# A cross-attention kernel on one core: GpSimd adds beta in two parts, and VectorE takes a residual ahead of a centring

## The chip, the cores and the metric

The kernel runs on 1 core of one Trainium2 chip. The metric is device time in microseconds (us). All times of the trace are counted from the start of the span of one profiled execution.

## The reference

```python
def _L0_xattn_ref(emb, latent, Wq, bq, Wk, bk, Wv, bv, gamma, beta):
    EPS = 1e-06
    q = jnp.einsum('bte,ef->btf', emb, Wq) + bq
    k = jnp.einsum('bml,le->bme', latent, Wk) + bk
    v = jnp.einsum('bml,le->bme', latent, Wv) + bv
    scale = 1.0 / jnp.sqrt(jnp.asarray(E, dtype=q.dtype))
    w = jnp.einsum('bte,bme->btm', q, k) * scale
    w = jax.nn.softmax(w, axis=1)
    pred = jnp.einsum('btm,bme->bte', w, v)
    x = pred + emb
    mu = jnp.mean(x, axis=-1, keepdims=True)
    var = jnp.var(x, axis=-1, keepdims=True)
    return (x - mu) * jax.lax.rsqrt(var + EPS) * gamma + beta
```

`emb` is x, 16 batches of 512 x 512 float32; `latent` is the context, 16 batches of 120 x 256. The softmax runs over the 512 tokens of a batch. The last three lines are a layer norm over the 512 features of a token.

## The kernel before

A batch's 512 tokens lie on 128 partitions as four units of 128 tokens x 512 features. Each engine has its own program, written out by hand; semaphores are all that ties them together, and an engine that waits holds up everything behind it in its program.

The loop has one step for each batch. In step s TensorE works on three batches at once:

- it turns x of batch s (L371; x must have landed), which ScalarE copies to `xT` (L501);
- it multiplies the probabilities of batch s-2 by its v, four products of 128 tokens each (L390), into the banks a, b, a, b. Products 1 and 2 stand between the two halves of the turning, 3 and 4 behind it. Product 4 writes the bank that VectorE's second residual reads, and waits for it;
- it multiplies contexts with the combined query and key matrix into `cg_ps` (L352, from which ScalarE makes `gT`, L496), computes v of batch s-1 (L363, which waits for the third residual, since it writes bank a), in steps 3, 5, 7, 9 and 11 turns a pair of contexts (L336, which waits for `gT`), and computes the scores of batch s (L400).

In the same step VectorE makes the softmax of batch s-1 ready (L680 to L689), takes the four residuals of batch s-2 (L721: product + x, with a sum), scales the softmax (L694, L696), makes the low half of the probabilities (L700, `prob_low`, which waits for ScalarE's high half, L513, `prob_high`), copies v (L706) and takes the statistics of unit 4 (L727, L729). Unit 4 of batch s-3 it normalises by itself: `center` (L746) subtracts the mean and multiplies by gamma, `rescale` (L754) multiplies by the inverse deviation and adds beta. In the first steps it also computes key products, `key_dot` (L675) and `key_sum` (L670).

Units 1 to 3 take another way. ScalarE squares them (L528) and GpSimd turns the sums into an inverse deviation and a `shift` (L940 to L958, `finish_statistics`). A step later ScalarE's `normalise` (L534) applies both: the first unit between the exponential (L506) and `prob_high`, the second and third behind the copies of `xT`. GpSimd multiplies each by gamma (L925, `times_gamma`) and adds beta to all three in one instruction (L931, `plus_beta`). Then its statistics of the next batch follow. So GpSimd's program for one batch is gamma, gamma, gamma, beta, statistics.

All DMAs are issued by SP, in one queue. In its loop a store of a batch (L295) waits for GpSimd (`pool_out`) and VectorE (`dve_out`), and the next load of x (L262), into a ring of four buffers, stands behind that store in SP's program. In step s that load is x of batch s+1. Stores leave from a ring of three buffers.

The last two batches divide the units otherwise (`pool_units`: 1 and 2 on GpSimd, the rest on VectorE) and are stored unit by unit.

Of the kernel before, what the change touches and what calls it, by code (L numbers as in the profile page):

```python
# [5 lines left out]
P = 128  # L6
# [3 lines left out]
ALU = mybir.AluOpType  # L10
# [5 lines left out]
ORING = 3  # L16
# [22 lines left out]
def cross_attention(nc, x, ctx_in, Wq, bq, Wk, bk, Wv, bv, gamma, beta, out):  # L39
    B, T, E = x.shape  # L40
# [11 lines left out]
    def pool_units(b):  # L52

        return {B - 2: 1, B - 1: 2}.get(b, 3)

    def units_before(b):
        return sum(pool_units(i) for i in range(b))
# [15 lines left out]
    def dve_units_before(b):  # L73
        return sum(dve_units(i) for i in range(b))
# [5 lines left out]
    with ExitStack() as stack:  # L80
        def sb(name, shape, dt=F32):
            return stack.enter_context(nc.sbuf_tensor(name, shape, dt))
# [4 lines left out]
        def sem(name):  # L87
            return stack.enter_context(nc.semaphore(name))
# [13 lines left out]
        beta_all = sb("beta_all", [P, E])  # L102
# [27 lines left out]
        obuf = sb("obuf", [P, ORING, RJ, E])  # L130
# [119 lines left out]
        pool_gamma = sem("pool_gamma")  # L250
        pool_out = sem("pool_out")
# [7 lines left out]
        @block.sync  # L259
        def _(sp):  # L260
            def load_x(b):
                sp.dma_start(xbuf[:, b % XRING], x[b].rearrange("(p j) e -> p j e", j=RJ)).then_inc(x_in[b % XRING], 16)  # L262

            def load_ctx(g):
                first = g * IN_GROUP
                sp.dma_start(ctx_nat[:, first:first + IN_GROUP, 0:L],
                             ctx_in[first:first + IN_GROUP].rearrange("b m l -> m b l")).then_inc(ctx_in_sem[g], 16)

            sp.dma_start(wk_nat[:], Wk.rearrange("(c p) f -> p c f", p=P)).then_inc(wk_in, 16)
            for h in range(2):  # L270
                sp.dma_start(wq_nat[:, 2 * h:2 * h + 2], Wq.rearrange("(c p) f -> p c f", p=P)[:, 2 * h:2 * h + 2])\
                    .then_inc(wq_in[h], 16)
            load_ctx(0)
            sp.dma_start(bk_all[:], bk.partition_broadcast(P)).then_inc(bk_in, 16)
            sp.dma_start(bq_all[:], bq.partition_broadcast(P)).then_inc(bq_in, 16)
            load_x(0)
            load_ctx(1)
            sp.dma_start(wv[:], Wv.rearrange("(c p) e -> p c e", p=P)).then_inc(wv_in, 16)
            load_ctx(2)
            load_ctx(3)  # L280
            sp.dma_start(bv_all[:], bv.partition_broadcast(P)).then_inc(bv_in, 16)
            load_x(1)
            load_x(2)
            sp.dma_start(gamma_all[:], gamma.partition_broadcast(P)).then_inc(gamma_in, 16)
            sp.dma_start(beta_all[:], beta.partition_broadcast(P)).then_inc(beta_in, 16)
            load_x(3)

            for s in range(4, B + 2):
                if s < B:
                    sp.wait_ge(y_done, RJ * (s - 4) + RJ)  # L290
                    load_x(s)
                b = s - 4
                sp.wait_ge(pool_out, b + 1)
                sp.wait_ge(dve_out, dve_units_before(b + 1))
                sp.dma_start(out[b].rearrange("(p j) e -> p j e", j=RJ), obuf[:, b % ORING])\  # L295
                    .then_inc(stored[b % ORING], 16)

            for b in range(B - 2, B):
                for j in (2, 0, 3, 1) if b == B - 1 else (1, 2, 3, 0):
                    sp.wait_ge(last_out[b - B + 2][j], 1)  # L300
                    sp.dma_start(out[b].rearrange("(p j) e -> p j e", j=RJ)[:, j], obuf[:, b % ORING, j])\
                        .then_inc(last_stored, 16)
            for k in range(ORING):
                sp.wait_ge(stored[k], 16 * len(range(k, B - 2, ORING)))
            sp.wait_ge(last_stored, 16 * 2 * RJ)
# [322 lines left out]
        def _(dve):  # L628
# [63 lines left out]
            def softmax_scale(b):  # L692
                dve.wait_ge(probs_done, b + 1)
                dve.reciprocal(s_rec[:], s_sum[:]).then_inc(rec_done, 1)  # L694
                dve.wait_ge(rec_done, b + 1)
                dve.tensor_scalar(s_by[:], s_rec[:], PROB_SCALE, None, ALU.mult).then_inc(by_done, 1)  # L696
# [17 lines left out]
            def residual(b, j):  # L714
                dve.wait_ge(pv_done, RJ * b + j + 1)
                if j == 0:
                    if b >= ORING:
                        dve.wait_ge(stored[b % ORING], 16 * (b // ORING))
                    if b >= 2:
                        dve.wait_ge(shift_done, b - 1)  # L720
                dve.scalar_tensor_tensor(obuf[:, b % ORING, j, :], y_bank(b, j), back_y[:], xbuf[:, b % XRING, j, :],  # L721
                                         ALU.mult, ALU.add, accum_out=y_sum[:, b % 2, j:j + 1]).then_inc(y_done, 1)
# [116 lines left out]
            for s in range(2, B):  # L839
                y, norm = s - 2, s - 3  # L840
                softmax_bias(s - 1)
                residual(y, 0)
                softmax_scale(s - 1)
                if norm >= 0:
                    center(norm, RJ - 1, norm + 1)
                residual(y, 1)
                probs_to_low(s - 1)
                residual(y, 2)
                residual(y, 3)
                if norm >= 0:  # L850
                    rescale(norm, RJ - 1)
                copy_v(s - 1)
                statistics(y)
                if s % 2 == 1 and (s + 3) // 2 < PAIRS:
                    ctx_to_low((s + 3) // 2)
                v_to_low(s - 1)
                if s == B - 1:
                    copy_v(s)
                    v_to_low(s)
                if s < IN_GROUP:  # L860
                    key_dot(s)
                if s - 1 in (1, 2, 3):
                    key_sum(s - 1)
# [24 lines left out]
        def _(pool):  # L888
# [36 lines left out]
                    pool.tensor_tensor(obuf[:, b % ORING, j, :], obuf[:, b % ORING, j, :], gamma_all[:], ALU.mult)\  # L925
                        .then_inc(pool_gamma, 1)

            def plus_beta(b):
                n = pool_units(b)
                pool.wait_ge(pool_gamma, units_before(b + 1))  # L930
                pool.tensor_tensor(obuf[:, b % ORING, 0:n, :], obuf[:, b % ORING, 0:n, :],  # L931
                                   beta_all[:].unsqueeze(1).broadcast_to([P, n, E]), ALU.add)\
                    .then_inc(pool_out if b < B - 2 else last_out[b - B + 2][0], 1)

            def finish_statistics(b):
# [25 lines left out]
            for s in range(2, B + 1):  # L961
                if s == 3:
                    key_multiply(s)
                if s >= 3:
                    times_gamma(s - 3)
                    plus_beta(s - 3)
                finish_statistics(s - 2)
            finish_statistics(B - 1)
            times_gamma(B - 2)
            plus_beta(B - 2)  # L970
            for j in range(pool_units(B - 1)):
                pool.wait_ge(norm_done, units_before(B - 1) + j + 1)
                pool.tensor_tensor(obuf[:, (B - 1) % ORING, j, :], obuf[:, (B - 1) % ORING, j, :], beta_all[:],
# [22 lines left out]
```

## Time and profile before

| | |
|---|---|
| median of 3 runs | 228.85 us (227.89 to 231.82) |
| profiled execution | 228.07 us |
| its span | 226.2 us |
| TensorE matmul busy | 190.5 us, 84% |
| VectorE busy | 169.3 us, 75% |
| ScalarE busy | 162.7 us, 72% |
| GpSimd busy | 142.0 us, 63% |
| TensorE's granted clock, mean | 0.957 of full speed |

The busy shares are means over an opening of some 40 us, the loop, and a tail from about 203 us on. In a timeline a row is one instruction, or several alike that follow one another: its start, its length, the engine, the line of the kernel, the operation, output <- inputs, sizes, and the count. In brackets stands how long the engine was idle before it, and what ended that. Matmuls are pipelined, so the row of one may reach into the next.

### The profile page before, as it was taken

Reading aid. Unit: us, or ns where it says so; the run is one execution under the profiler, and the core shown is the slowest. Engines: PE = TensorE matmul, PEld = TensorE weight load, DVE = VectorE, ACT = ScalarE, POOL = GpSimd, SP = SyncE. Lnnn points to the kernel's source line nnn. Section 1 sums busy time; section 2 is a strip of 40 time slices with the busy share of each in tenths; the row PEclk is TensorE's granted clock in tenths of the full one; section 3 lists DMA queues with packets and bytes.
Section 4 is the critical chain, followed back from the end, with each engine's and each line's share of the span. In section 5 each row is a group of like instructions: output and inputs, shape, how many; then the busy total and the mean of one; then the engine's idle time right before and its main releaser. Section 6 shows DMA issues by size and latency. Waiting matters only on the chain.

```text
span 226.2 us, 3278 instructions
## 1 busy us (share of the span) xinstructions
PE 190.5 (84%) x1003; PEld 117.6 (52%) x1003; DVE 169.3 (75%) x403; ACT 162.7 (72%) x336; POOL 142.0 (63%) x149
## 2 busy tenths in 40 slices
PE   6994998899996999999999999999999969696100
PEld 6993655465554565656565656555656535342000
DVE  0698138979899896959695969586958686879891
ACT  2745638378968797978797879787978876748730
POOL 1010005103994969696969696969696969698991
PEclk9999599999999999999999999999999999999855
DMA  5999940014018090909090909090909090404175
GB/s 220 315 313 250 398 198 1 3 14 172 0 81 293 0 346 28 352 22 351 23 355 17 352 19 351 23 336 36 348 26 352 19 351 25 185 0 187 67 294 197
DMA packets 9277, 39.14 MB, mean 173 GB/s; under 512 B 812, under 2 KB 2732, under 8 KB 5420
## 3 DMA queue, kind: packets, MB, share of 16 engines
q1 hardware_dynamic: 9260, 38.93, 49.0%
q8 instruction: 8, 0.13, 0.2%
q14 instruction: 9, 0.07, 0.1%
HBM read 22.15 MB, written 16.78 MB: 172 GB/s over the span
## 4 chain that ended last, share of the span: by engine, by line
PE 40%; POOL 16%; DVE 14%; ACT 9%; issue 8%; DMA 7%; SPq 2%; POOLq 1%; ACTq 0%; DVEq 0%
PE s_ps L400 16%; DMA ctx_nat<-in_ctx 7%; POOL obuf L925 7%; PE xT_ps L371 6%; POOL obuf L931 5%; PE a_ps L363 5%; PE a_ps L390 4%; PE b_ps L390 4%; DVE obuf L721 4%; PE cg_ps L352 4%; ACT xT L501 3%; ACT obuf L534 2%; POOL rstd L954 2%; ACT prob_part L513 2%; DVE obuf L746 2%
## 5 line engine op out<-in xcount | busy, mean ns | idle before, releaser
L925 POOL TENSOR_TENSOR obuf<-obuf,gamma_all 128x512 f32<-128x512 f32 x43 | 54.2, 1276 | 24.9 <-ACT obuf L534 24.9
L400 PE MATMUL s_ps<-xT,gT 128*120 128x512 f32 x128 | 58.9, 604 | 0.0
L931 POOL TENSOR_TENSOR obuf<-obuf,beta_all 128x1536 f32<-128x1536 f32 (+1 forms) x15 | 49.6, 3306 | 1.2
L501 ACT ACTIVATE xT<-xT_ps 128x512 f32<-128x512 f32 x64 | 34.6, 593 | 17.3 <-PE xT_ps L371 17.3
L534 ACT ACTIVATE obuf<-obuf,shift,rstd 128x512 f32<-128x512 f32 x43 | 33.4, 813 | 9.0 <-POOL shift L958 9.0
L371 PEld LDWEIGHTS xT_ps<-ident,xbuf 128*128 128x128 f32 x256 | 30.1, 142 | 15.1 <-issue 8.0
L371 PE MATMUL xT_ps<-ident,xbuf 128*128 128x128 f32 x256 | 34.0, 275 | 3.8 <-ACT xT L501 3.8
L400 PEld LDWEIGHTS s_ps<-xT,gT 128*120 128x120 f32 x128 | 23.5, 188 | 25.6 <-issue 23.7
L528 ACT ACTIVATE square_junk<-obuf,y_sum 128x512 f32<-128x512 f32 x46 | 32.8, 716 | 0.0
L390 PE MATMUL b_ps<-v_part,prob_part 120*128 120x512 f16 x90 | 24.5, 381 | 4.9 <-DVE obuf L721 4.9
L680 DVE TENSOR_REDUCE s_max<-s_ps 120x1 f32<-120x512 f32 x16 | 11.0, 689 | 20.3 <-PE s_ps L400 20.3
L390 PE MATMUL a_ps<-v_part,prob_part 120*128 120x512 f16 x90 | 24.4, 379 | 1.7 <-DVE v_part L711 0.9
L363 PE MATMUL a_ps<-wv_part,ctxT 128*120 128x512 f16 x90 | 22.0, 381 | 3.4 <-DVE obuf L721 3.1
L721 DVE SCALAR_TENSOR_TENSOR obuf<-a_ps,back_y,xbuf 128x512 f32<-128x512 f32 x30 | 22.4, 745 | 3.0 <-PE a_ps L390 3.0
L721 DVE SCALAR_TENSOR_TENSOR obuf<-b_ps,back_y,xbuf 128x512 f32<-128x512 f32 x30 | 22.3, 745 | 0.0
L352 PE MATMUL cg_ps<-ctxT,qk_part 128*128 128x240 f16 x156 | 18.1, 266 | 0.0
L390 PEld LDWEIGHTS b_ps<-v_part,prob_part 120*128 120x128 f16 x90 | 7.6, 97 | 19.1 <-DVE obuf L721 11.7
L706 DVE SCALAR_TENSOR_TENSOR a_ps<-a_ps,onto_v,bv_scaled 120x512 f32<-120x512 f32 x15 | 11.4, 758 | 8.2 <-PE a_ps L363 8.2
L954 POOL TENSOR_TENSOR rstd<-var_eps,minus_half 128x4 f32<-128x4 f32 x16 | 16.3, 1020 | 1.3 <-POOL var_eps L940 0.2
L352 PEld LDWEIGHTS cg_ps<-ctxT,qk_part 128*128 128x128 f16 x156 | 15.2, 98 | 3.5
L363 PEld LDWEIGHTS a_ps<-wv_part,ctxT 128*120 128x120 f16 x90 | 11.2, 133 | 10.1 <-issue 4.0
L700 DVE SCALAR_TENSOR_TENSOR prob_part<-s_ps,s_by,prob_part 120x512 f16<-120x512 f32 x16 | 12.0, 750 | 4.0 <-ACT prob_part L513 3.7
(142 smaller groups left out, 277.2 us busy)
## 6 DMA issues: line engine op xcount, KB each, us to landing
xbuf<-in_x SPq DMA_DIRECT2D x16, 1024.0 KB, 7.4
out<-obuf SPq DMA_DIRECT2D x14, 1024.0 KB, 4.8
out<-obuf SPq DMA_DIRECT2D x8, 256.0 KB, 2.8
ctx_nat<-in_ctx SPq DMA_DIRECT2D x4, 480.0 KB, 14.0
wq_nat<-in_L_xattn_Wq SPq DMA_DIRECT2D x2, 512.0 KB, 5.0
wk_nat<-in_L_xattn_Wk SPq DMA_DIRECT2D x1, 512.0 KB, 3.7
wv<-in_L_xattn_Wv SPq DMA_DIRECT2D x1, 512.0 KB, 14.3
bk_all<-in_L_xattn_bk SPq DMA_DIRECT2D x1, 256.0 KB, 7.6
```

What stands on the lines that cost most here:

```text
L352: mm = pe.matmul(ps[:, i * 2 * M:(i + 1) * 2 * M], qk_part[:, of_w, c, e * P:(e + 1) * P], ctxT[:, pair % 3, of_ctx, c, :], start=(n == 0) ...
L363: mm = pe.matmul(v_bank(b)[0:M, :], ctxT[:, b // 2 % 3, of_ctx, c, at:at + M], wv_part[:, of_w, c, :], start=(n == 0), stop=(n == len(step ...
L371: mm = pe.transpose(xT_ps[e % 2][:, j, :], xbuf[:, b % XRING, j, e * P:(e + 1) * P], ident[:])
L390: mm = pe.matmul(y_bank(b, j), prob_part[:, b % 2, of_p, j * P:(j + 1) * P], v_part[:, b % 2, of_v, :], start=(n == 0), stop=(n == len(PAS ...
L400: mm = pe.matmul(s_ps[0:M, :], gT[:, b // 2 % 2, e, b % 2 * M:(b % 2 + 1) * M], xT[:, e, :], start=(e == 0), stop=(e == EC - 1))
L501: act.activation(xT[:, e, :].rearrange("p (j q) -> p j q", q=P), xT_ps[e % 2][:], ACT.Copy)\
L528: act.activation(junk[:, j], obuf[:, b % ORING, j, :], ACT.Square, scale=-float(E), bias=y_sum[:, b % 2, j:j + 1], accum_out=square_sum[:, ...
L534: act.activation(obuf[:, b % ORING, j, :], obuf[:, b % ORING, j, :], ACT.Identity, bias=shift[:, b % 2, j:j + 1], scale=rstd[:, b % 2, j:j ...
L721: dve.scalar_tensor_tensor(obuf[:, b % ORING, j, :], y_bank(b, j), back_y[:], xbuf[:, b % XRING, j, :], ALU.mult, ALU.add, accum_out=y_sum ...
L925: pool.tensor_tensor(obuf[:, b % ORING, j, :], obuf[:, b % ORING, j, :], gamma_all[:], ALU.mult)\
L931: pool.tensor_tensor(obuf[:, b % ORING, 0:n, :], obuf[:, b % ORING, 0:n, :], beta_all[:].unsqueeze(1).broadcast_to([P, n, E]), ALU.add)\
L954: pool.tensor_tensor(rstd[:, k], var_eps[:], minus_half[:], ALU.pow).then_inc(rstd_done, 1)
```

## The change

GpSimd's addition of beta, which was one instruction for all three units of a batch, becomes two: units 1 and 2 at the old place, and unit 3 behind the next batch's statistics. `pool_out` counts both, so SP waits for twice the count. On VectorE the second residual and the centring change places.

```diff
@@ SP, the loop over stores and loads
                 b = s - 4
-                sp.wait_ge(pool_out, b + 1)
+                sp.wait_ge(pool_out, 2 * (b + 1))
                 sp.wait_ge(dve_out, dve_units_before(b + 1))
@@ VectorE, step s
                 softmax_scale(s - 1)
+                residual(y, 1)
                 if norm >= 0:
                     center(norm, RJ - 1, norm + 1)
-                residual(y, 1)
                 probs_to_low(s - 1)
@@ GpSimd
-            def plus_beta(b):
-                n = pool_units(b)
-                pool.wait_ge(pool_gamma, units_before(b + 1))
-                pool.tensor_tensor(obuf[:, b % ORING, 0:n, :], obuf[:, b % ORING, 0:n, :],
-                                   beta_all[:].unsqueeze(1).broadcast_to([P, n, E]), ALU.add)\
+            def plus_beta(b, first, end):
+                pool.wait_ge(pool_gamma, units_before(b) + end)
+                pool.tensor_tensor(obuf[:, b % ORING, first:end, :], obuf[:, b % ORING, first:end, :],
+                                   beta_all[:].unsqueeze(1).broadcast_to([P, end - first, E]), ALU.add)\
                     .then_inc(pool_out if b < B - 2 else last_out[b - B + 2][0], 1)
@@ GpSimd, its loop
                 if s >= 3:
                     times_gamma(s - 3)
-                    plus_beta(s - 3)
+                    plus_beta(s - 3, 0, 2)
                 finish_statistics(s - 2)
+                if s >= 3:
+                    plus_beta(s - 3, 2, 3)
             finish_statistics(B - 1)
             times_gamma(B - 2)
-            plus_beta(B - 2)
+            plus_beta(B - 2, 0, 1)
```

GpSimd's program in the middle of the loop, before: from one batch's gamma to the next batch's. The names in brackets are the semaphores that an instruction waits for.

```order
L925 TENSOR_TENSOR obuf<-obuf,gamma_all 128x512 [waits norm_done] x3
L931 TENSOR_TENSOR obuf<-obuf,beta_all 128x1536 [waits pool_gamma]
L940 TENSOR_SCALAR var_eps<-square_sum 128x3 [waits squares_done]
L947 TENSOR_SCALAR neg_mean<-y_sum 128x3 [waits dve_out,centered,norm_done]
L951 TENSOR_TENSOR var_eps<-mean_var,eps_all 128x1 [waits aggr_done]
L954 TENSOR_TENSOR rstd<-var_eps,minus_half 128x4 [waits var_ready]
L958 TENSOR_TENSOR shift<-neg_mean,rstd 128x3 [waits mean_negated,rstd_done]
L925 TENSOR_TENSOR obuf<-obuf,gamma_all 128x512 [waits norm_done] x3
```

The same place after the change (the file is one line shorter there):

```order
L925 TENSOR_TENSOR obuf<-obuf,gamma_all 128x512 [waits norm_done] x3
L930 TENSOR_TENSOR obuf<-obuf,beta_all 128x1024 [waits pool_gamma]
L939 TENSOR_SCALAR var_eps<-square_sum 128x3 [waits squares_done]
L946 TENSOR_SCALAR neg_mean<-y_sum 128x3 [waits dve_out,centered,norm_done]
L950 TENSOR_TENSOR var_eps<-mean_var,eps_all 128x1 [waits aggr_done]
L953 TENSOR_TENSOR rstd<-var_eps,minus_half 128x4 [waits var_ready]
L957 TENSOR_TENSOR shift<-neg_mean,rstd 128x3 [waits mean_negated,rstd_done]
L930 TENSOR_TENSOR obuf<-obuf,beta_all 128x512 [waits pool_gamma]
L925 TENSOR_TENSOR obuf<-obuf,gamma_all 128x512 [waits norm_done] x3
```

The statistics moved ahead of one third of beta, and that third moved between them and the next batch's gamma.

VectorE's program in a step of the loop, as a piece of the difference, from the scaling of the softmax to the third residual:

```order
 L696 TENSOR_SCALAR s_by<-s_rec 120x1
-L746 SCALAR_TENSOR_TENSOR obuf<-obuf,mean_var,gamma_ps 128x512
-L721 SCALAR_TENSOR_TENSOR obuf,y_sum<-b_ps,back_y,xbuf 128x512
+L721 SCALAR_TENSOR_TENSOR obuf,y_sum<-b_ps,back_y,xbuf 128x512
+L746 SCALAR_TENSOR_TENSOR obuf<-obuf,mean_var,gamma_ps 128x512
 L700 SCALAR_TENSOR_TENSOR prob_part<-s_ps,s_by,prob_part 120x512
 L721 SCALAR_TENSOR_TENSOR obuf,y_sum<-a_ps,back_y,xbuf 128x512
```

The residual from bank b (L721) and the centring (L746) changed places; both stand ahead of `prob_low` (L700) as before.

## Rows read from the trace of the kernel before

**Rows 1.** Timeline of GpSimd in step 8, and its second gamma seven steps later.

```profile
115.40 1.27 POOL L925 TENSOR_TENSOR obuf<-obuf,gamma_all 128x512 f32<-128x512 f32 x1 [0.93 <-ACT obuf L534]
117.65 2.51 POOL L925 TENSOR_TENSOR obuf<-obuf,gamma_all 128x512 f32<-128x512 f32 x2 [0.98 <-ACT obuf L534]
120.24 3.46 POOL L931 TENSOR_TENSOR obuf<-obuf,beta_all 128x1536 f32<-128x1536 f32 x1
123.78 0.20 POOL L940 TENSOR_SCALAR var_eps<-square_sum 128x3 f32<-128x3 f32 x1
...
125.59 0.20 POOL L958 TENSOR_TENSOR shift<-neg_mean,rstd 128x3 f32<-128x3 f32 x1
...
196.75 2.51 POOL L925 TENSOR_TENSOR obuf<-obuf,gamma_all 128x512 f32<-128x512 f32 x2 [0.98 <-ACT obuf L534]
```

**Rows 2.** Timeline of ScalarE in step 8: the first normalise, then the other two.

```profile
114.51 0.81 ACT L534 ACTIVATE obuf<-obuf,shift,rstd 128x512 f32<-128x512 f32 x1 [0.24 <-POOL shift L958]
...
116.75 1.52 ACT L534 ACTIVATE obuf<-obuf,shift,rstd 128x512 f32<-128x512 f32 x2
```

**Rows 3.** Timeline of TensorE: where steps 5, 8 and 15 begin, a wait, four products.

```profile
77.85 1.04 PE L371 MATMUL xT_ps<-ident,xbuf 128*128 128x128 f32 x8
...
108.00 0.60 PE L336 MATMUL cg_ps<-ident,ctx_nat 120*128 120x120 f32 x4 [0.33 <-ACT gT L496]
...
111.88 1.04 PE L371 MATMUL xT_ps<-ident,xbuf 128*128 128x128 f32 x8
...
113.40 0.81 PE L390 MATMUL b_ps<-v_part,prob_part 120*128 120x512 f16 x3
114.05 1.04 PE L371 MATMUL xT_ps<-ident,xbuf 128*128 128x128 f32 x8
114.92 0.81 PE L390 MATMUL a_ps<-v_part,prob_part 120*128 120x512 f16 x3
116.06 0.82 PE L390 MATMUL b_ps<-v_part,prob_part 120*128 120x512 f16 x3 [0.32 <-DVE obuf L721]
...
190.03 1.04 PE L371 MATMUL xT_ps<-ident,xbuf 128*128 128x128 f32 x8
```

**Rows 4.** Timeline of VectorE: centring and second residual in step 8, prob_low in step 15.

```profile
114.58 0.75 DVE L746 SCALAR_TENSOR_TENSOR obuf<-obuf,mean_var,gamma_ps 128x512 f32<-128x512 f32 x1
115.25 0.74 DVE L721 SCALAR_TENSOR_TENSOR obuf<-b_ps,back_y,xbuf 128x512 f32<-128x512 f32 x1
...
195.03 0.75 DVE L700 SCALAR_TENSOR_TENSOR prob_part<-s_ps,s_by,prob_part 120x512 f16<-120x512 f32 x1 [0.88 <-ACT prob_part L513]
```

**Rows 5.** SP's x(10) load; then x loads' us to landing: x(7,9,10,11,13,15).

```profile
124.11 0.43 SPq L262 DMA_DIRECT2D xbuf<-in_x  x1
...
xbuf<-in_x SPq DMA_DIRECT2D x1, 1024.0 KB, 7.7
...
xbuf<-in_x SPq DMA_DIRECT2D x1, 1024.0 KB, 7.5
...
xbuf<-in_x SPq DMA_DIRECT2D x1, 1024.0 KB, 6.9
...
xbuf<-in_x SPq DMA_DIRECT2D x1, 1024.0 KB, 8.4
...
xbuf<-in_x SPq DMA_DIRECT2D x1, 1024.0 KB, 8.6
...
xbuf<-in_x SPq DMA_DIRECT2D x1, 1024.0 KB, 7.3
```

**Rows 6.** Timeline of steps 3 and 4: a GpSimd, a VectorE and two TensorE rows.

```profile
62.58 3.45 POOL L931 TENSOR_TENSOR obuf<-obuf,beta_all 128x1536 f32<-128x1536 f32 x1
...
64.06 2.26 DVE L675 SCALAR_TENSOR_TENSOR key_junk<-ctx_nat,w_row 120x257 f32<-120x257 f32 x1
...
69.35 0.82 PE L390 MATMUL a_ps<-v_part,prob_part 120*128 120x512 f16 x3 [0.79 <-DVE obuf L721]
...
71.23 0.82 PE L390 MATMUL b_ps<-v_part,prob_part 120*128 120x512 f16 x3 [1.06 <-DVE obuf L721]
```

## The prediction

> **What bounds the kernel now.** I read the page first (engine shares and the chain that ended last), then the timelines of GpSimd, ScalarE, TensorE and VectorE over step 8 of the loop, and last the DMA queue. The page shows TensorE as the busiest engine, but the timelines show that it does not set the pace. Write T(s) for the moment at which TensorE starts to turn x of batch s; T(8) is 111.88 [rows 3]. In step 8 ScalarE's first normalise starts at 114.51, and its bracket says that it waited 0.24 us for GpSimd's `shift` [rows 2]. The second normalise starts 2.24 later, at 116.75. GpSimd's second and third gamma units start at 117.65, 0.90 behind that. Beta starts at 120.24, 2.59 later, and lasts 3.46; the statistics start at 123.78 and `shift` ends at 125.79, 2.01 later [rows 1]. Then the next step's normalise can go. That ring is 2.24 + 0.90 + 2.59 + 3.54 + 2.01 = 11.28 us, and 0.03 more to the next normalise make 11.31. From 117.65 to the same instruction seven steps later, at 196.75, are 79.10 us, so 11.30 each [rows 1]: the ring of GpSimd and ScalarE sets every step. TensorE runs into it: in every step its fourth product waits for VectorE's second residual. Products that wait for nothing follow one another at 0.65 us (113.40 to 114.05), the fourth started 1.14 behind the third (114.92 to 116.06), so it stood 0.49; in steps that turn a pair of contexts it stood another 0.33 for ScalarE's gT [rows 3]. So TensorE alone would need two steps in about 22.60 - 0.98 - 0.33 = 21.3 us.
>
> **Beta in two parts.** A unit of 128x512 costs 1.27, read from gamma, which is the same operation [rows 1], three together 3.46, so each unit beyond the first costs 1.09 and two units 2.36. The ring loses 1.10 us and becomes about 10.2 a step, shorter than TensorE's 10.6. The third unit costs 1.27, so GpSimd works 0.17 more per batch. It lies behind `shift`, where GpSimd stood idle 0.93 us for the first normalise [rows 1]; the rest, 0.3 us, only moves the first gamma unit, and between the first and second gamma there is another 0.98 us of idle time [rows 1]. It costs nothing while that idle time is there; without it, 1.27 a step, which would undo the saving.
>
> What is late next is the store, since `pool_out` now counts two per batch, and SP issues the next x load behind that store. Before, the load that follows was issued at 124.11, 0.41 behind the end of beta and T(8) + 12.23 [rows 5]. After, with `shift` no longer late, the first normalise starts at T + 2.63 - 0.24 = 2.39, the second at 4.63, the gamma pair at 5.53, beta at 8.12, its two units end at 10.48, the statistics start 0.08 later and end at 12.57, the third unit ends 1.27 + 0.08 later at 13.92, and the load is issued at T + 14.33. Two of the gaps of 0.08 follow an instruction that the next one no longer depends on and may close, so the bounds are 14.1 and 14.33; I take 14.2, TensorE's own wake-up in it. The load is thus about 2 us later in its step, and steps become shorter.
>
> This load, issued in step s, is x(s+1). So there is a new ring of two steps: T(s+1) is not before T(s-1) + 14.2 + landing. The landings are not equal: x(10) took 6.9 us, x(7), x(9), x(11), x(13), x(15) took 7.7, 7.5, 8.4, 8.6 and 7.3 [rows 5]. With 6.9 the ring takes 21.1, and TensorE's own 21.3 hides it. With the odd batches' landings it takes 21.5 to 22.8 and binds. Then T(15) = T(5) + 5 x 14.2 + 39.5 (the five landings) = T(5) + 110.5. Before, it was 190.03 - 77.85 = 112.18 [rows 3]. **This gains 1.7 us over ten steps**, where the shorter GpSimd ring promised 11. Bounds: 105.4 if no load binds (ten steps without 0.49, three without 0.33, step 14 without the 0.9 below), and 114.0 if every odd landing is 8.6.
>
> What is late in these landings decides. I expect them to stay: they are a property of the transfer, not of its wait. The Trainium skill (DMA: Bandwidth & Descriptors, Queues, rings and completion order) says that each of the 16 DMA engines takes turns, packet by packet, among the queue rows that have work; by it an instruction fetch that meets a load holds up one sixteenth of it, and the sum would stay as above as long as fetches still fall into the odd loads. No row here shows which packets delayed these landings.
>
> The same store frees an output buffer. It stands ahead of the load in the queue, and the buffer is first wanted by a first residual in the step in which that load's x is turned, behind the turning; so nothing waits for it that the load does not hold up first. No DMA is added, and SP's order is unchanged.
>
> **Step 4, once.** VectorE's `key_dot` at 64.06 took 2.26 us and ended at 66.32, 0.29 behind GpSimd's beta (62.58 to 66.03) [rows 6]. I read it as blocked by that beta, which now ends 1.09 earlier. Behind it stand the key sum, the softmax and the residuals, for which TensorE waited 0.79 and 1.06 us at 69.35 and 71.23. The second residual also moves up by a centring (0.67). Together that would be 1.76 of 1.85; prob_low and the third residual behind it give back some, so I take **1.6** (bounds: 0.7, if only the move counts, and 1.85).
>
> The Trainium skill (SBUF — State Buffer, SBUF: two separate sides) says that a VectorE instruction with two SBUF inputs and a GpSimd instruction share a port pair as an exclusive lock, whoever starts first keeping it. By that rule the gain is the 1.09 of the shorter beta; if the long `key_dot` had another cause, step 4 would bring 0.7 and the total would be 0.9 us longer. The trace agrees so far as the end at 66.32 goes, not more.
>
> **The second residual ahead of the centring.** Nothing is added; two VectorE instructions of 0.75 change places. The residual starts at T + 2.70 instead of 3.37 [rows 4]; product 4 starts 0.81 behind its start (115.25 to 116.06), so at T + 3.51, before TensorE gets there (114.92 + 0.65 is T + 3.69): the 0.49 goes. The centring is needed only by the rescale behind the fourth residual, on VectorE itself, and prob_low stands behind both in either order, so its price is nothing; if prob_high came so early that prob_low waited for the centring, 0.67 a step.
>
> **Step 15 and the tail.** VectorE's prob_low at 195.03 waited 0.88 for ScalarE [rows 4], which waited for `shift`; behind it TensorE waits to compute v. With `shift` early this goes: **0.9** (bounds 0 and 0.9). In the tail GpSimd's statistics wait for squares, so the shorter beta brings nothing; the third unit of batch 12 stands ahead of the gamma units of batch 13, 1.27 where 0.93 was idle: **0.3 lost**. Batch 13's third unit is now after statistics on the same engine, which changes its order and not its length (another 0.17 at most).
>
> **Sum.** 1.6 + 1.7 + 0.9 - 0.3 = 3.9 us. The profiled execution took 228.07 us (span 226.2), so 224.2; the median shown is 228.85, 0.8 above it.
>
> **The rivals.**
> Loads stay hidden: the odd landings come near 6.9, or stores leave sooner, and TensorE sets the pace. For it: x(10) needed 6.9. Against: five of five odd ones were longer. Then 112.18 - 105.4 = 6.8 instead of 1.7, 9.0 in all: **219.1**.
> Loads take nearly everything: every odd landing at 8.6. Then 114.0 - 112.18 = 1.8 is lost, 0.4 gained in all: **227.7**. For it: two of five are that long, and a later load has more of the step's other traffic beside it.
> Slower: the same ring, but with landings that grow because the load is moved. Its place is TensorE's wait for x at the start of each odd step, its price one us per step pair for each us of landing. It decides from a mean landing of 8.7 on (71.0 + 43.4 = 112.18 + 2.2); at 9.6 the time is 228.07 + 4.6 = **232.7**. Against: the queue holds one store and one load per step, as before.
> The change does nothing: the ring had another cause. It would leave 228. Against: seven steps at exactly 11.30, and the sum of its rows meets that.
>
> **How the numbers follow.** Loads bind as measured, 221.5 to 226.5: 0.58; hidden: 0.18; nearly everything taken, or nothing done: 0.19; slower: 0.05. The range goes from the hidden case to the case that takes nearly everything, 219.1 to 227.7. A difference under 2% (4.6 us) is about what a measurement of this kernel can tell from none. The forecast is 1.7% faster; of its own case about four in ten lie beyond 2%, so with the hidden case: faster 0.42, within 2% 0.53, slower 0.05.
>
> **What would show it.** Right: ScalarE's first normalise no longer waits for `shift`; product 4 no longer waits for VectorE; `key_dot` ends near 65.2; x loads are issued about 14 us behind the T before, and TensorE waits for x at odd steps, most at x(11) and x(13). Wrong: no wait for x (then the time is near 219), odd landings over 8.7, or a first gamma unit that pushes the second.

## The result, and the profile after

| | before | changed |
|---|---|---|
| median | 228.84 us (227.89 to 231.82) | 220.02 us (218.04 to 221.65) |
| ratio | | 0.960 (0.951 to 0.969) |
| profiled execution, its span | 228.07, 226.2 us | 219.85, 218.0 us |
| TensorE's granted clock, mean | 0.957 | 0.963 |

The ratio, here and in the experiments, leaves out executions that were clearly slower than the others of their kernel, such as 231.82 before, 221.65 after and one of 406.18 us in E9 below.

The change makes the kernel 4.0% faster. The forecast was 224.2 us with a range of 219.1 to 227.7: the time lies in the range, but near its low end, beside the rival "loads stay hidden" (219.1). So the direction was right, and one term of the sum was wrong by some 3.5 us. That the time lies in the range is owed to this rival, which set the range's low end, and not to the forecast's own case.

Timeline of TensorE after the change: where steps 3, 5 and 8 begin, the last two products of step 8, steps 12 and 15, and the first of the product block behind step 15.

```profile
53.10 1.04 PE L371 MATMUL xT_ps<-ident,xbuf 128*128 128x128 f32 x8
...
75.45 1.04 PE L371 MATMUL xT_ps<-ident,xbuf 128*128 128x128 f32 x8
...
107.68 1.04 PE L371 MATMUL xT_ps<-ident,xbuf 128*128 128x128 f32 x8
...
110.72 0.81 PE L390 MATMUL a_ps<-v_part,prob_part 120*128 120x512 f16 x3
111.37 0.81 PE L390 MATMUL b_ps<-v_part,prob_part 120*128 120x512 f16 x3
...
150.72 1.09 PE L371 MATMUL xT_ps<-ident,xbuf 128*128 128x128 f32 x8 [0.33 <-DMA xbuf<-in_x]
...
182.41 1.10 PE L371 MATMUL xT_ps<-ident,xbuf 128*128 128x128 f32 x8
...
188.04 1.48 PE L363 MATMUL a_ps<-wv_part,ctxT 128*120 128x512 f16 x6 [1.07 <-DVE obuf L721]
...
194.08 0.81 PE L390 MATMUL a_ps<-v_part,prob_part 120*128 120x512 f16 x3
```

The fourth product starts 0.65 behind the third (110.72 to 111.37), as products do that wait for nothing; before it stood 0.49 there [rows 3]. At step 8 TensorE starts without a bracket: x(8) is there. At step 12 a new wait has come, for x(12).

Timelines after the change of GpSimd, ScalarE and VectorE in step 8, one fence for each, the last with `prob_low` of step 15.

```profile
110.85 1.28 POOL L925 TENSOR_TENSOR obuf<-obuf,gamma_all 128x512 f32<-128x512 f32 x1 [0.54 <-ACT obuf L534]
113.10 2.52 POOL L925 TENSOR_TENSOR obuf<-obuf,gamma_all 128x512 f32<-128x512 f32 x2 [0.97 <-ACT obuf L534]
115.56 2.37 POOL L930 TENSOR_TENSOR obuf<-obuf,beta_all 128x1024 f32<-128x1024 f32 x1
118.02 0.20 POOL L939 TENSOR_SCALAR var_eps<-square_sum 128x3 f32<-128x3 f32 x1
...
119.81 0.19 POOL L957 TENSOR_TENSOR shift<-neg_mean,rstd 128x3 f32<-128x3 f32 x1
119.97 1.28 POOL L930 TENSOR_TENSOR obuf<-obuf,beta_all 128x512 f32<-128x512 f32 x1
```

```profile
109.95 0.82 ACT L534 ACTIVATE obuf<-obuf,shift,rstd 128x512 f32<-128x512 f32 x1
...
112.18 1.54 ACT L534 ACTIVATE obuf<-obuf,shift,rstd 128x512 f32<-128x512 f32 x2
```

```profile
110.37 0.74 DVE L721 SCALAR_TENSOR_TENSOR obuf<-b_ps,back_y,xbuf 128x512 f32<-128x512 f32 x1
111.04 0.74 DVE L746 SCALAR_TENSOR_TENSOR obuf<-obuf,mean_var,gamma_ps 128x512 f32<-128x512 f32 x1
...
186.49 0.74 DVE L700 SCALAR_TENSOR_TENSOR prob_part<-s_ps,s_by,prob_part 120x512 f16<-120x512 f32 x1
```

Beta of two units takes 2.37, the third 1.28, and ScalarE's first normalise has lost its bracket [rows 2]: the normalise now starts 2.27 behind TensorE's start (109.95 - 107.68), which is 120.27 in the next step (T(9) is 118.00), and `shift` ends at 120.00. So this ring is 0.27 us from binding again in odd steps (in even ones, as step 8, `shift` ends 0.88 ahead). `prob_low` in step 15 has lost its 0.88 [rows 4].

Before, the ring of GpSimd and ScalarE set each step. Now the loop runs up to T(11) at TensorE's own pace, 10.95 and 10.33 in turn, 21.28 for two steps (T(7) is 96.73); the prediction had put it at 21.3.

Where the 8.2 us of the profiled execution went, from [rows 3], the rows above and the same timelines (before, T(3) is 53.80 and the product block starts at 202.63):

| stretch | before | changed | gained | forecast |
|---|---|---|---|---|
| start to T(3), where the code is the same | 53.80 | 53.10 | 0.70 | 0 |
| T(3) to T(5) | 24.05 | 22.35 | 1.70 | 1.6 |
| T(5) to T(15) | 112.18 | 106.96 | 5.22 | 1.7 |
| T(15) to the product block | 12.60 | 11.67 | 0.93 | 0.9 |
| the rest of the span | 23.57 | 23.92 | -0.35 | -0.3 |

Three of the four forecast terms came within 0.1 us. The fourth, the ten steps of the loop, is where the prediction said that loads of x would bind. From T(5) to T(15) the granted clock was 1.00 of full speed in both traces (the higher level, 2.4 GHz), so the 5.22 are not the clock's; up to T(3) it was 0.94 before and 0.97 after, on average.

SP's timeline after the change, in step 8: the store, and the load of x(10).

```profile
121.27 0.34 SPq L295 DMA_DIRECT2D out<-obuf  x1
121.66 0.43 SPq L262 DMA_DIRECT2D xbuf<-in_x  x1
```

The DMA view of three stretches, around the loads of x(11), x(12) and x(13). The last number of a load's line is its time from issue to landing. A line q8 or q14 says how many packets of instructions the chip fetched in the stretch, their size (0.02 or 0.01 MB), and their time as a share of 16 DMA engines.

```profile
q1 hardware_dynamic: 288, 2.10, 74.8%
...
xbuf<-in_x SPq DMA_DIRECT2D x1, 1024.0 KB, 6.9
```

```profile
q14 instruction: 1, 0.01, 0.2%
...
xbuf<-in_x SPq DMA_DIRECT2D x1, 1024.0 KB, 7.7
```

```profile
q8 instruction: 1, 0.02, 0.6%
...
xbuf<-in_x SPq DMA_DIRECT2D x1, 1024.0 KB, 8.0
```

The load is issued at T(8) + 13.98 (121.66 - 107.68); the prediction took 14.2. x(7) to x(11), odd and even, landed 6.89 to 6.94 after their issue, not 7.5 to 8.4 [rows 5]. They land 0.35 to 0.39 before TensorE turns them: just in time. The longest were x(12) and x(13), 7.75 and 8.02, and TensorE begins each of the steps 12 to 15 only 0.04 behind the landing of its x. The waits view after the change has these waits of TensorE's weight loads for x in one line (total us, times, longest):

```profile
PEld xT_ps L371 <- DMA xbuf<-in_x: 6.0, 11, 1.2
```

Eleven waits, but a weight load runs ahead of its matmul, and most of this lies under matmuls that still run. The four steps from T(11) to T(15) took 43.13; in E3 below, where no load is waited for, the same four took 41.91. So the waits cost 1.22 us.

### The profile page after: what moved, and what is told of

The parts are those of the page before. It is cut to its first block and busy times, and to the rows that moved or that the text cites. A ratio compares the mean times of both kernels' runs of the same rounds, so it can differ in the third digit from the quotient of the medians.

```text
span 218.0 us, 3292 instructions
## 1 busy us (share of the span) xinstructions
PE 189.2 (87%) x1003; PEld 118.1 (54%) x1003; DVE 167.4 (77%) x403; ACT 161.7 (74%) x336; POOL 143.0 (66%) x163
## 5 line engine op out<-in xcount | busy, mean ns | idle before, releaser
L930 POOL TENSOR_TENSOR obuf<-obuf,beta_all 128x512 f32<-128x512 f32 (+1 forms) x29 | 52.2, 1801 | 0.1
L371 PEld LDWEIGHTS xT_ps<-ident,xbuf 128*128 128x128 f32 x256 | 29.5, 141 | 15.6 <-DMA xbuf<-in_x 6.0
L721 DVE SCALAR_TENSOR_TENSOR obuf<-a_ps,back_y,xbuf 128x512 f32<-128x512 f32 x30 | 22.4, 745 | 4.3 <-PE a_ps L390 3.2
L721 DVE SCALAR_TENSOR_TENSOR obuf<-b_ps,back_y,xbuf 128x512 f32<-128x512 f32 x30 | 22.3, 744 | 0.0
L390 PEld LDWEIGHTS b_ps<-v_part,prob_part 120*128 120x128 f16 x90 | 8.6, 97 | 11.3 <-DVE obuf L721 1.1
L520 ACT ACTIVATE v_part<-a_ps 120x512 f16<-120x512 f32 x15 | 8.9, 595 | 7.6 <-DVE a_ps L706 7.6
```

Of the source, the lines that this page charges most:

```text
L371: mm = pe.transpose(xT_ps[e % 2][:, j, :], xbuf[:, b % XRING, j, e * P:(e + 1) * P], ident[:])
L390: mm = pe.matmul(y_bank(b, j), prob_part[:, b % 2, of_p, j * P:(j + 1) * P], v_part[:, b % 2, of_v, :], start=(n == 0), stop=(n == len(PAS ...
L930: pool.tensor_tensor(obuf[:, b % ORING, first:end, :], obuf[:, b % ORING, first:end, :], beta_all[:].unsqueeze(1).broadcast_to([P, end - f ...
```

## The experiments

The theory after the result: three bounds lie close together. The GpSimd ring (11.30 a step) and product 4 behind the second residual both had to go; behind them stands TensorE (21.28 per two steps), and 0.35 us behind that the ring through the load of x. The rival of the prediction's kind: the landing is fixed, so that the load ring binds whatever TensorE does.

### E1 and E2: each part alone

E1 is the changed kernel with VectorE's old order, E2 the kernel before with the new order on VectorE alone:

```
E1 (on the changed kernel)              E2 (on the kernel before)
  softmax_scale(s - 1)                    softmax_scale(s - 1)
- residual(y, 1)                        + residual(y, 1)
  if norm >= 0:                           if norm >= 0:
      center(norm, RJ - 1, norm + 1)          center(norm, RJ - 1, norm + 1)
+ residual(y, 1)                        - residual(y, 1)
```

> The changed kernel with the old order on VectorE: only beta is in two parts. Theory (two steps take the longest of three: the GpSimd ring, now 20.4; TensorE with its waits; the load ring, 14.0 + 6.9): product 4 waits 0.49 again in every step, two steps take about 22.2, T(5) to T(15) about 110.8 us against 107.0, and step 4 gives back 0.7: about 224.4 us. Rival (the shorter ring alone made the gain): about 220 us.

E1 took 225.09 us, ratio 0.990 (0.981 to 0.999). T(5) to T(15) took 110.48. The waits view of E1 keeps the line of the fourth product:

```profile
PE b_ps L390 <- DVE obuf L721: 4.6, 13, 0.8
```

> The kernel before with only the second residual ahead of the centring. Theory: the GpSimd ring of 11.30 still sets every step, product 4 no longer waits and the time comes back as a wait elsewhere: T(5) to T(15) 112 to 113 us, total about 228 us. Rival (the 0.49 us of each step are saved by themselves): about 223 us.

E2 took 228.47 us, ratio 1.005 (0.998 to 1.011), T(5) to T(15) 112.67. Its waits view:

```profile
ACT obuf L534 <- POOL shift L958: 11.2, 14, 1.6
...
PE a_ps L363 <- DVE obuf L721: 7.8, 7, 2.0
...
PE cg_ps L336 <- ACT gT L496: 2.2, 6, 0.6
```

Both came as expected. In E2 the time that product 4 no longer waits is waited a little later, in front of v of the next batch (7.8 us in 7 waits) and for gT: nothing is gained while GpSimd's ring sets the step. In E1 the ring is gone, but product 4 still waits for the residual, 4.6 us in 13 steps. So the parts bring about 1% and nothing, and together 4%: each took away one of two bounds, 11.30 and 11.05 a step (E1's 110.48 over ten). Some 1.0 us of the 110.48 is a late load: x(13) of E1 landed 8.68 behind its issue, and the step to T(13) took 11.77 where its like took 10.80.

### E3 and E4: the load ahead of the store

SP issues the load of x(s+1) before it waits for the store, as soon as the batch that held the buffer has its residuals. The loop's body in both:

```
+ sp.wait_ge(y_done, RJ)
+ load_x(4)
  for s in range(4, B + 2):
-     if s < B:
-         sp.wait_ge(y_done, RJ * (s - 4) + RJ)
-         load_x(s)
+     if s + 1 < B:
+         sp.wait_ge(y_done, RJ * (s - 3) + RJ)
+         load_x(s + 1)
      b = s - 4
```

> The changed kernel with SP issuing the load of x(s+1) ahead of the store that it stood behind. Theory: loads then land long before their step, TensorE alone sets the pace, the waits for x in steps 12 to 15 (1.1 us) go: T(5) to T(15) 105.9 us, about 218.8 us. Rival (the x waits only hide another wait of the same length): about 219.9 us.

E3 (on the changed kernel) took 218.79 us (216.69 to 219.91), ratio 0.964 (0.953 to 0.975), T(5) to T(15) 105.71. The loads of the loop leave some 8 us earlier than in the changed kernel, and land 9.7 us or more before they are wanted. The prediction's bound for ten steps in which no load binds was 105.4. One line of what E3's trace says of the load's line of code (min, median, max over 16 loads; the longest is of the opening):

```profile
DMA to landing us min/median/max: 4.6/4.8/17.3
```

> The kernel before with SP issuing the load of x(s+1) ahead of the store. Theory: the GpSimd ring sets the pace and x landed 1.3 us or more ahead of its step already: no change, about 228 us. Rival (late loads cost the kernel before too): up to 2 us faster.

E4 (on the kernel before) took 228.68 us, ratio 1.000 (0.995 to 1.004), T(5) to T(15) 112.18, to the hundredth what it was.

So before the change the load ring was hidden, and in the changed kernel it costs 106.96 - 105.71 = 1.25 us over the ten steps. Also, a load that isn't issued behind a store lands in 4.8 us, not 6.9. The 2.1 between them is the store in front of it.

### E5: the load later, the store where it was

```
  sp.wait_ge(y_done, RJ * (s - 4) + RJ)
+ if s >= 5:
+     sp.wait_ge(pool_gamma, units_before(s - 4) + 1)
  load_x(s)
```

> The changed kernel with each x load also waiting for the first gamma unit of the next batch, which ends at about T(s) + 4.5. Theory (a ring over the x load): the load of x(s+1) is issued at T(s) + 4.5 and takes 6.9 or more, so every step takes at least 11.4 us, TensorE waits for x in every step, T(5) to T(15) about 115 us, about 228 to 230 us. Rival (the load has room): about 220 us.

E5 took 221.66 us (220.46 to 222.25), ratio 0.974 (0.965 to 0.983), T(5) to T(15) 107.68: the expectation failed. SP's timeline of E5 around the load of x(10), and the landing of that load in the DMA view:

```profile
122.17 0.34 SPq L297 DMA_DIRECT2D out<-obuf  x1
123.55 0.33 SPq L262 DMA_DIRECT2D xbuf<-in_x  x1
```

```profile
xbuf<-in_x SPq DMA_DIRECT2D x1, 1024.0 KB, 5.9
```

The loads of x(7) to x(11) left 0.9 to 1.5 us later than in the changed kernel, but they landed 5.6 to 5.9 us after their issue instead of 6.9. From the store's issue to the load's landing it is 7.23 here (122.17 to 129.40) and 7.30 in the changed kernel (121.27 to 128.57); over x(6) to x(11) it is 7.14 to 7.69 here and 7.27 to 7.33 there. The two megabytes end at nearly the same time behind the store's start; whether the load is issued 0.4 us behind it or 1.3 to 1.9 hardly matters. A delay of the load alone is thus not paid us for us; for a delay of the store see E9.

### E9: the store later

The wait of E5, put ahead of the store:

```
  sp.wait_ge(pool_out, 2 * (b + 1))
+ if b + 1 < B - 2:
+     sp.wait_ge(pool_gamma, units_before(b + 1) + 1)
```

> The changed kernel in which each store waits for the first gamma unit of the next batch, so that store and load both leave later, at about T(s) + 4.5 and 4.9. With only the load later it landed 5.2 to 6.0 us behind its issue and not 6.9: what counts may be the store's issue. Theory (the two transfers together take about 7.3 us from the store's issue): the load of x(s+1) lands at T(s) + 11.8, each step takes about 11.85, T(5) to T(15) about 118 us, about 230 us. Rival (landing shrinks again or has room): about 222 us.

E9's profiled execution took 236.92 us, the ratio is 1.035 (1.026 to 1.044), T(5) to T(15) 121.0. The direction was right, the size was not: it is 14.0 us over the changed kernel in the loop, more than the theory gave. Timelines of E9 in step 8: TensorE's start, GpSimd's first gamma, SP, and TensorE's next start.

```profile
112.99 1.09 PE L373 MATMUL xT_ps<-ident,xbuf 128*128 128x128 f32 x8 [0.75 <-DMA xbuf<-in_x]
...
116.22 1.28 POOL L927 TENSOR_TENSOR obuf<-obuf,gamma_all 128x512 f32<-128x512 f32 x1 [1.51 <-ACT obuf L536]
...
117.56 0.34 SPq L297 DMA_DIRECT2D out<-obuf  x1
117.95 0.43 SPq L262 DMA_DIRECT2D xbuf<-in_x  x1
...
125.07 1.10 PE L373 MATMUL xT_ps<-ident,xbuf 128*128 128x128 f32 x8 [1.54 <-DMA xbuf<-in_x]
```

The gamma unit that the store waits for follows TensorE's start of its own step: T(8) + 3.23. The load thus leaves at T(8) + 4.96, lands 7.08 later and lets T(9) begin. With this wait the ring closes over one step, as the expectation had it, where the changed kernel's closes over two: eight of the eleven landings are 6.92 to 6.95 (the others 7.07, 7.08 and 8.33), which makes a step 4.96 + 6.92 + 0.04 = 11.92, and nine of the ten steps take 11.92 to 12.08. The expectation had 11.85; the tenth step, behind the landing of 8.33, took 13.34. The total missed by more, since the steps from T(3) to T(5) took 1.6 and the end behind T(15) 1.3 longer than in the changed kernel as well. That shows the load ring through the store: pushed far enough, it sets every step. Store and load leave 2.90 us later than in the changed kernel (x(s+1) at T(s-1) + 16.88 against T(s-1) + 13.98), and two steps take 23.85 instead of 21.28: the delay less some 0.35 of room. The landing is still 6.9, so what it has over E3's 4.8 goes with the store in front, not with the place in the step.

### E6: beta in two instructions at the old place

The kernel before with beta in two instructions, of two units and of one, both ahead of the statistics; VectorE keeps its old order. As a difference from the changed kernel's GpSimd program:

```
  plus_beta(s - 3, 0, 2)
+ plus_beta(s - 3, 2, 3)
  finish_statistics(s - 2)
- if s >= 3:
-     plus_beta(s - 3, 2, 3)
```

> The kernel before with beta in two instructions, both still ahead of the statistics, and the old order on VectorE. Theory: the ring grows by the second instruction's fixed cost, about 0.1 us a step (11 steps); key_dot gets in after the first part and ends 1.1 us earlier, so step 4 gives 1.1: about 228 us. Rival (key_dot is long for another reason): key_dot still ends near 66.3, about 229.2 us.

E6 took 228.45 us, ratio 0.999 (0.994 to 1.004), T(5) to T(15) 112.62. It gains nothing, and E1 (110.48) differs from it only in the place of the third unit, so it is this place that shortens the ring, not the split. E6 also decides step 4: T(3) to T(5) took 22.85, 1.20 less than before. GpSimd's beta and VectorE's `key_dot`, of E6 and then of the changed kernel:

```profile
61.48 3.81 POOL L930 TENSOR_TENSOR obuf<-obuf,beta_all 128x1024 f32<-128x1024 f32 x2
...
63.10 1.06 DVE L675 SCALAR_TENSOR_TENSOR key_junk<-ctx_nat,w_row 120x257 f32<-120x257 f32 x1
```

```profile
61.77 2.35 POOL L930 TENSOR_TENSOR obuf<-obuf,beta_all 128x1024 f32<-128x1024 f32 x1
...
63.34 1.07 DVE L675 SCALAR_TENSOR_TENSOR key_junk<-ctx_nat,w_row 120x257 f32<-120x257 f32 x1
...
68.63 0.82 PE L390 MATMUL b_ps<-v_part,prob_part 120*128 120x512 f16 x3
```

The other three `key_dot` of each of these traces take 0.42. With one instruction of three units this one took 2.26 and ended 0.29 behind it [rows 6]. In the changed kernel it takes 1.07 and ends at 64.41, 0.29 behind the 64.12 at which the instruction of two units ends. In E6 GpSimd works on, with a second beta instruction, until 65.29, and `key_dot` still ends at 64.16, some 0.3 behind the end of the first (61.48 + 2.36 = 63.84). So it waits here for the end of the one GpSimd instruction that runs when it starts, and the second does not get ahead of it. The fourth product of step 4, whose row showed a wait of 1.06 [rows 6], starts at 68.63 in the changed kernel without a bracket. The Trainium skill (SBUF — State Buffer, SBUF: two separate sides) has the port pair of the two engines as an exclusive lock, held for a whole instruction by whoever starts first, between a GpSimd instruction that reads SBUF and a VectorE instruction with two SBUF inputs, which `key_dot` is; these ends agree.

### E7: another place for the instruction fetches

The changed kernel with 26 more transposes on TensorE in a gap of the opening, which shift its program and with it the points at which instructions are fetched:

```
  turn_x(0, 2)
+ keep_warm(26, b_ps)
  turn_x(0, 3)
```

> The changed kernel with 26 extra transposes on TensorE in a gap of the opening (their output is overwritten), so that later instruction fetches of TensorE come some 4 us earlier or later against the steps. Theory (a fetch of 16 KB inside a load makes that load land 0.8 to 1.7 us later): other loads than x(12) and x(13) are late; if x(7), x(9) or x(11) are, T(5) to T(15) grows from 107.0 to 108 to 110 us. Loads without a fetch inside take 6.9. Rival (fetches do not matter): landings as in the changed kernel, 107.0.

E7 took 217.26 us (216.19 to 220.09), ratio 0.950 (0.939 to 0.960), T(5) to T(15) 106.71. The opening was 3.1 us shorter than in the changed kernel's profile (T(3) at 49.98), so the totals tell little here. Whether the added transposes did that is open: from 18 to 30 us the granted clock was 1.00 against 0.86 in the changed kernel, and E3 had 1.00 there without them. The landings do. DMA view around x(13), and around x(12), of E7:

```profile
q1 hardware_dynamic: 288, 2.10, 69.1%
...
xbuf<-in_x SPq DMA_DIRECT2D x1, 1024.0 KB, 6.9
```

```profile
q14 instruction: 1, 0.01, 0.2%
...
xbuf<-in_x SPq DMA_DIRECT2D x1, 1024.0 KB, 7.8
```

The fetch of 0.02 MB has left x(13), and x(13) lands in 6.9 instead of 8.0; the fetch on q14 still meets x(12), which still takes 7.8. But two other loads, x(6) and x(8), now have a fetch of 0.02 MB between issue and landing and took 7.10 and 6.93, against the expectation of 0.8 us or more on top. A fetch can make a load late and need not.

### E8, E10 and E11: loads first and the centring later

E8 is E3 with VectorE's centring moved behind the fourth residual, right ahead of the rescale that needs it:

```
  residual(y, 1)
- if norm >= 0:
-     center(norm, RJ - 1, norm + 1)
  probs_to_low(s - 1)
  ...
  if norm >= 0:
+     center(norm, RJ - 1, norm + 1)
      rescale(norm, RJ - 1)
```

> The changed kernel with loads ahead of stores, and the centring behind the fourth residual, right ahead of the rescale. Theory: as with loads first (218.8 us), and in steps 14 and 15 the third residual comes 0.34 us earlier, which TensorE waits for there: about 218.1 us. Rival (prob_low is held by ScalarE, not by the centring): as with loads first.

E8 took 217.94 us (217.62 to 218.10), ratio 0.954 (0.947 to 0.961), T(5) to T(15) 105.33. Where the changed kernel shows a wait of 1.07 in front of v in steps 14 and 15, E8 in step 14 shows this, in TensorE's timeline:

```profile
175.81 1.48 PE L365 MATMUL a_ps<-wv_part,ctxT 128*120 128x512 f16 x6 [0.76 <-DVE obuf L723]
```

E10 is the changed kernel again, E11 is E8 again, on one chip.

> The changed kernel as it is, on the same chip as the next one. Expected: 219 to 221 us, with a spread of some us between runs from the opening and from late x loads.

> Loads ahead of stores and the centring behind the fourth residual, beside the changed kernel on the same chip. Theory (x waits of about 1.1 us and two waits of 0.3 us in steps 14 and 15 go): 1.5 to 2 us below the changed kernel. Rival: the same time as the changed kernel.

E10 took 220.70 us (219.85 to 222.00), ratio 0.968 (0.963 to 0.973), E11 219.11 us (218.04 to 219.93), ratio 0.959 (0.954 to 0.964): 1.6 us between the medians, as expected, with intervals that still touch. The loads and the centring bring what the accounts say, some 0.7%.

E10 adds one thing. Its T(5) to T(15) took 108.8, not 106.96, with the same program: x(11) landed 8.86 after its issue and x(13) 8.07. SP's row of the load of x(11), and TensorE's start of that step:

```profile
131.95 1.82 SPq L262 DMA_DIRECT2D xbuf<-in_x  x1
...
140.85 1.09 PE L371 MATMUL xT_ps<-ident,xbuf 128*128 128x128 f32 x8 [1.46 <-DMA xbuf<-in_x]
```

SP took 1.82 us to issue it, instead of 0.43. A fetch of 0.02 MB was running then: it began 0.80 before the issue and took 1.47, which is its share in the DMA view from 131 to 133 us. The line of the fetch:

```profile
q8 instruction: 1, 0.02, 4.6%
```

A second such issue, of x(9), stands in SP's timeline of E2:

```profile
113.60 1.26 SPq L262 DMA_DIRECT2D xbuf<-in_x  x1
```

In the eight kernels in which the load stands 0.4 us behind the store, eight loads of the loop were issued while a fetch of 0.02 MB that had begun earlier still ran, and their issue took 0.47 to 1.82 us; that of all the others took 0.43 to 0.44. The slow issue alone does not make a late landing: E2's x(9) landed 7.02 behind its issue. Of E10's x(11), fifteen of sixteen parts had landed at 7.34 and the last at 8.86. The changed kernel has only 0.35 us of room there, so such a landing is paid by TensorE. E11, with its loads 9.5 us ahead, took 105.33 in the loop, the same as E8.

## Why the prediction was right, and where it was not

**The ring of GpSimd and ScalarE** was right: the steps went from 11.30 to TensorE's own pace, and `shift` no longer holds up the first normalise (the few waits that are left, 0.8 us in 3, lie ahead of T(5) and behind T(15)). E6 beside E1 shows that it is the third unit's place that did it. Beta's prices (2.36 forecast, 2.37 measured; 1.27 and 1.28) and the load's issue (14.1 to 14.33 as bounds, 13.98 to 14.03 measured) came from rows and held; the small gaps behind instructions that the next doesn't depend on closed, so the issue lies just under the lower bound.

**Step 4, step 15 and the tail** came at 1.70, 0.93 and -0.35 against 1.6, 0.9 and -0.3. The reading of `key_dot` as blocked by beta is borne out by E6. Of the 1.70 in step 4, beta alone brings 1.22 (E1) and the residual alone 0.48 (E2), against 1.09 and 0.67 in the prediction.

**The second residual** was right in its place and incomplete in its worth. The 0.49 went. But E1 and E2 show that neither part does without the other: without the residual the loop gains 1.7 us of the 5.22 (some 2.7 without E1's one late load, by estimate), and the residual alone gains nothing.

**The failed step** is the sentence "I expect them to stay: they are a property of the transfer, not of its wait", in the term of the ten steps. The ring, T(s+1) not before T(s-1) + issue + landing, exists: from T(12) on TensorE starts 0.04 us behind each landing, E3 without the ring is 1.25 us shorter, and in E9 it sets every step. Its landing was mis-sized: the five odd landings were put at 39.5 us as before, and were 35.8 (6.89, 6.94, 6.92, 8.02 and 7.00). By the prediction's own formula with the measured values, 5 x 14.0 + 35.8 = 105.8, as much as TensorE takes by itself over these steps (105.71 in E3), so the load hardly binds. The gain was 5.22 instead of 1.7; the 3.5 us between them are most of the 4.35 by which the forecast missed the profiled execution, and the opening's 0.7 is nearly all of the rest.

Why the landings were not a property of the transfer: of 6.9 us only 4.8 belong to the load, the rest to the store ahead of it (E3, E5). What came on top of 6.9 went with instruction fetches. DMA view of the kernel before, around x(11):

```profile
q8 instruction: 1, 0.02, 0.6%
...
xbuf<-in_x SPq DMA_DIRECT2D x1, 1024.0 KB, 8.4
```

The stretch is 9 us long, so 0.6% of 16 engines are 0.9 us of one engine for this one fetch. The landing events of this load fit that: fifteen of its sixteen parts had landed 6.88 us after the issue, the last at 8.39. Counted over the loads of x(5) to x(15) of the eight kernels that issue the load 0.4 us behind the store (before, changed, E1, E2, E6, E7, E9, E10), 53 had no fetch of 8 or 16 KB between issue and landing: 52 of them took 6.89 to 7.13, and the 53rd is E10's x(11), at whose issue a fetch was still running (as at that of six of the 52). 35 had one: 22 of them took 7.3 to 8.7, and 13 took 6.89 to 7.11. In the kernel before, E2 and E6, which keep its pace, x(11) and x(13) are late each time (8.14 to 8.63); with shorter steps and a later load the same program points fall elsewhere. That the odd loads of the loop were the late ones went with the timing of that kernel.

The link of fetch and late landing is a count over many loads and one shift (E7), not more: no run took a fetch away and left everything else where it was, and what decides which fetch delays a load is open. The Trainium skill (DMA: Bandwidth & Descriptors, Queues, rings and completion order) has each DMA engine take turns, packet by packet, among its queue rows. The one late part of sixteen agrees with that; which fetches do harm no run here derives from it.

**The chances.** Faster by more than 2% was given 0.42 and within 2% 0.53, and the hidden loads 0.18. "Five of five odd ones were longer" counted as evidence for the loads, where it was evidence for one timing of them. The trace of before showed the way out: x(10) at 6.9 behind a store like all others.

Of the signs that the prediction named, four came: no wait for `shift`, none for the residual, `key_dot` at its short length, and loads 14 us behind T. The fifth came at other steps: TensorE waits for x most at x(12), and at x(11) not at all.

## What to carry to other kernels

When two bounds lie close together, neither part of a change shows what it is worth alone (E1 1%, E2 nothing, both 4%): cost the parts together, and name the third bound behind them, here 21.28 of TensorE and a load with 0.35 us of room. A landing time that is read from a trace contains what is queued in front of the transfer and what happens to cross it, so ask which part goes along when the transfer is moved: a load that depends on no store should be issued ahead of it (6.9 to 4.8 us, and 9.5 us of room). And follow what a wait that is put into an experiment waits for through the next step: it can close a ring of its own, as E9's, over one step where the kernel's closes over two.

## What the runs showed of the hardware

- A load of 1 MB that SP issues 0.4 us behind a store of 1 MB lands 6.9 us after its issue; issued 1.3 to 1.9 us behind it (E5, x(6) to x(11)), 5.6 to 6.0; not behind one, 4.6 to 5.3 over the 44 loads of the four kernels with loads first.
- A single instruction fetch of 0.02 MB took 0.9 us of one DMA engine in the case shown (0.6% of 16 in 9 us) and 0.9 to 1.8 in the loops of the eight kernels (the longest in E1), and loads that one crossed landed up to 1.8 us later than the 6.9 of the others, some of them not later at all.
- SP took 0.47 to 1.82 us to issue the eight loads at whose issue a fetch of 0.02 MB still ran, and 0.43 to 0.44 for the others; behind the longest (E10), TensorE stood 1.46 us. That the fetch is the cause is not shown.
- A VectorE instruction that stood blocked by a GpSimd instruction went on behind that one, though GpSimd's next followed without a gap: `key_dot` ended 0.3 behind the first of two (seen once, E6).
